# Attention over keys: score tiles in two alternating pairs of banks, queries' keys placed by DMA

## The reference

```
# causal self-attention (fourth sublayer)
q, k, v = split(x @ W_attn + b_attn)            # 16 heads of 8
s = q k^T / (sqrt(8) * temperature) + slope_h * (key - query), key <= query
y = softmax(s) v ;  out = y @ W_proj + b_proj

# cross attention (fifth sublayer)
q = x @ Wq^T ; k, v = ctx @ Wk^T, ctx @ Wv^T    # 16 heads of 8
s = q k^T / sqrt(8), masked where mask[b, key] == 0
out = (softmax(s) v) @ Wo^T
```

## Time and profile before

| | us |
|---|---|
| median of three runs | 1710.38 |
| profiled execution | 1718.98 |
| its span | 1717.2 |
| TensorE (PE) busy | 1404.5 (82%) |
| VectorE (DVE) busy | 1283.2 (75%) |
| ScalarE (ACT) busy | 1015.6 (59%) |
| GpSimd (POOL) busy | 746.1 (43%) |

### The profile page before, as it was taken

How to read it: one execution, slowest core, us unless ns; L and a number is a source line. 1 busy time by engine, 2 the same in 40 slices (tenths; PEclk the granted TensorE clock), 3 DMA queues, 4 the chain that set the end, 5 groups by cost and what they waited for, 6 DMA issues and landing times.

```text
span 1717.2 us, 62575 instructions
## 1 busy us (share of the span) xinstructions
PE 1404.5 (82%) x26438; PEld 907.4 (53%) x26438; DVE 1283.2 (75%) x2645; ACT 1015.6 (59%) x1749; POOL 746.1 (43%) x1471
## 2 busy tenths in 40 slices
PE   4788788878885776777767777999999998989897
PEld 2455455555554443444334444666666666666676
DVE  2345556664453899899988886999999999999966
ACT  2465565666543444444456666777777777777755
POOL 1334334444243565766566664334343333223223
PEclk8688688898775678677655557999999999999999
DMA  7000000000000000000000000000000000000012
GB/s 189 2 2 2 2 3 2 2 3 2 2 2 2 20 15 21 14 15 15 16 1 2 1 1 2 2 3 3 2 3 3 15 15 22 15 22 15 3 32 69
DMA packets 28664, 24.22 MB, mean 14 GB/s; under 512 B 3676, under 2 KB 23906, under 8 KB 28386
## 3 DMA queue, kind: packets, MB, share of 16 engines
q1 hardware_dynamic: 28386, 20.21, 4.3%
HBM read 15.94 MB, written 4.19 MB: 12 GB/s over the span
## 4 chain that ended last, share of the span: by engine, by line
PE 29%; issue 27%; ACT 17%; POOL 17%; DVE 9%; SPq 0%; DMA 0%; POOLq 0%; ACTq 0%; DVEq 0%
PE keys_T L577 7%; ACT keys_pexp L662 5%; POOL gla_low L1102 4%; PE keys_E L473 3%; DVE cross_mx L338 3%; ACT ffn_hqT L1813 2%; POOL gla_yg L1126 2%; ACT keys_pT L644 2%; ACT xs L305 2%; PE keys_E L516 2%; PE ffn_OUT L1774 2%; POOL gla_sq L1119 2%; PE keys_O L584 2%; DVE cross_sums L946 2%; PE keys_S L319 1%
## 5 line engine op out<-in xcount | busy, mean ns | idle before, releaser
L644 ACT ACTIVATE keys_pT<-keys_T 128x512 f32<-128x512 f32 x256 | 152.3, 595 | 107.5 <-PE keys_T L577 104.0
L328 POOL TENSOR_SCALAR keys_spread<-keys_kT,keys_heads 128x512 f32<-128x512 f32 x128 | 86.7, 695 | 260.4 <-ACT keys_kT L608 260.4
L338 DVE TENSOR_REDUCE keys_mx<-keys_S 128x16 f32<-128x1024 f32 x128 | 156.5, 1222 | 39.7 <-PE keys_S L543 25.0
L577 PE MATMUL keys_T<-ident_sb,keys_pexp 128*128 128x128 f32 x1024 | 165.3, 284 | 22.5 <-ACT keys_pexp L662 18.5
L577 PEld LDWEIGHTS keys_T<-ident_sb,keys_pexp 128*128 128x128 f32 x1024 | 112.9, 141 | 98.4 <-ACT keys_pexp L662 50.5
L341 DVE TENSOR_TENSOR keys_pe_in<-keys_S,keys_mx 128x1024 f32<-128x1024 f32 x128 | 156.7, 1224 | 4.4
L1506 DVE COPY_PREDICATED gla_at<-gla_node,gla_GP 128x256 f32<-128x256 int32 x128 | 64.6, 505 | 103.8 <-ACT gla_at L1381 100.5
L662 ACT ACTIVATE keys_pexp<-keys_pe_in 128x1024 f32<-128x1024 f32 x128 | 134.2, 1049 | 0.0
L930 ACT ACTIVATE cross_pexp<-cross_pe_in 128x1024 f32<-128x1024 f32 x64 | 67.4, 1053 | 103.0 <-DVE cross_pe_in L341 102.9
L1119 POOL TENSOR_TENSOR gla_sq<-gla_o 128x512 f32<-128x512 f32 x32 | 33.3, 1039 | 217.9 <-ACT gla_o L1389 217.8
L697 DVE RECIPROCAL keys_rinv<-keys_O 128x128 f32<-128x128 f32 x128 | 120.4, 941 | 0.6 <-issue 0.2
(11 more groups left out here) (278 smaller groups left out, 3720.3 us busy)
## 6 DMA issues: line engine op xcount, KB each, us to landing
context<-in_ctx_T SPq DMA_DIRECT2D x32, 256.0 KB, 2.7
xs<-in_x SPq DMA_DIRECT2D x8, 512.0 KB, 7.3
out_x<-xs SPq DMA_DIRECT2D x16, 256.0 KB, 2.3
keys_mask_q<-keys_mask_b SPq DMA_DIRECT2D x64, 1.0 KB
keys_bias_right_f<-in_alibi_right SPq DMA_DIRECT2D x1, 512.0 KB, 4.0
ffn_w<-in_L_ffn_w_gate_T SPq DMA_DIRECT2D x1, 256.0 KB, 4.9
ffn_w<-in_L_ffn_w_up_T SPq DMA_DIRECT2D x1, 256.0 KB, 5.0
ffn_w<-in_L_ffn_w_down_T SPq DMA_DIRECT2D x1, 256.0 KB, 5.7
```

The lines of the kernel that those rows point to most:

```text
L328: nc.gpsimd.tensor_scalar(spread[:, :, :, j, :].rearrange("q t s k -> q (t s) k"), flat.rearrange("q (a k) -> q a k", k=SEQ), heads[:, j:j ...
L338: nc.vector.tensor_reduce(m, quads(S), X, ALU.max).then_inc(c["mx"], 1)
L577: last = nc.tensor.transpose(T[:, j * P:(j + 1) * P], pexp[:, t % 2, (4 * half + j) * P:(4 * half + j + 1) * P], sh.ident[:, :])
L644: nc.scalar.activation(pT[:, t % 2, 4 * half:4 * half + 4, :].rearrange("q n k -> q (n k)"), T[:, :], ACT.Copy).then_inc(c["pT"], 1)
```

## The change

`S` becomes two tiles of two banks, `S[0]` and `S[1]`, used by even and odd tiles. Scores wait for the subtraction of the tile two before. The scores are four products instead of eight: 64 rows (eight heads) by 64 output rows, 512 columns each. `spread` has OH = 8 places per row instead of 4; its zeros are written once, by GpSimd in the stage ffn, and stay. For each group SP copies each head's eight rows of `kT` into their place: 16 copies of eight rows of 2 KB, SBUF to SBUF. TensorE's first scores of a group wait for all 16, ScalarE's next writing of the same `kT` buffer too. GpSimd no longer multiplies. The mask is added by four products of 512 columns instead of eight of 256 (and copied to two rows instead of four), the bias by two of 512 instead of four of 256. VectorE's two instructions on the scores read the same number of elements, now contiguous. Clearing `vz` moves from the stage cross to ffn. The attribute `staging_read` in the diff is not called by anything.

```diff
+def zeroed(ap):
+    return ap.rearrange("q j n -> q (j n)")
+
+def place_heads(eng, sems, spread, rows, p):
+    for h in range(H):
+        eng.dma_start(spread[h * HD:(h + 1) * HD, p, h % OH, :], rows[h * HD:(h + 1) * HD, p, :]) \
+            .then_inc(sems[p], 16)
+
+def tensor_scores_halves(nc, S, still, spread, t, stop=True):
+    for s in range(2):
+        for a in range(2):
+            rows, at = slice(64 * a, 64 * a + 64), (2 * t + s) * SEQ
+            last = nc.tensor.matmul(S[s * SEQ:(s + 1) * SEQ, a * 512:(a + 1) * 512].rearrange("q (j k) -> q j k", k=SEQ),
+                                    still[rows, s * SEQ:(s + 1) * SEQ], spread[rows, :, at:at + SEQ],
+                                    start=True, stop=stop)
+    return last
+
+def vector_softmax_in_halves(nc, eng, c, S, mx, pe_in, g, t):
+    pp = t % 2
+    c.await_tile(eng, "scores", g, t)
+    x = S[pp][:, :].rearrange("q (h k) -> q h k", k=SEQ)
+    nc.vector.tensor_reduce(mx[:, pp, :], x, X, ALU.max).then_inc(c["mx"], 1)
...
-        spread = sb("spread", [P, 2, G, 2, QH, SEQ])
+        spread = sb("spread", [P, 2, OH, GW])
...
-        S = bank("S", 4)
+        S = [bank(f"S{i}", 2) for i in range(2)]
...
-        PREP, ZEROS = 9, 1
+        PREP, ZEROS = 9, 3
...
         @stage.on("sync")
         def _(sp):
             sp.wait_ge(c["prep"], PREP)
             sh.context_read(sp)
-            for n in range(NG):
+            def context(n):
                 g, p = NG + n, n % 2
                 if n >= 2:
                     c.free_group(sp, "v_done", g, 1)
                 sp.dma_start(cT[:, p, :], am["ctx_T"][:, bass.ds(n * GW, GW)]).then_inc(c[f"ctx{p}"], 16)
+
+            def masks(n):
+                g, p = NG + n, n % 2
                 if n >= 2:
                     c.free_tile(sp, "scores", g, G - 1)
-                for r in range(4):
-                    sp.dma_start(mask_q[32 * r:32 * r + 1, p, :, :, :].rearrange("q t s k -> q t (s k)"),
+                for a in range(2):
+                    sp.dma_start(mask_q[64 * a:64 * a + 1, p, :, :, :].rearrange("q t s k -> q t (s k)"),
                                  mask_b[n * G:(n + 1) * G, :]).then_inc(c[f"mask{p}"], 16)
+
+            context(0)
+            masks(0)
+            context(1)
+            masks(1)
+            for g in range(2 * NG):
+                c.await_nth(sp, "kT", g, 1, 1)
+                if g == 0:
+                    sp.wait_ge(c["zeros"], ZEROS)
+                c.free_tile(sp, "scores", g, G - 1)
+                place_heads(sp, (c["spread0"], c["spread1"]), spread, kT, g % 2)
+                if NG <= g < 2 * NG - 2:
+                    masks(g - NG + 2)
+                    context(g - NG + 2)
 
         @stage.on("gpsimd")
         def _(pool):
             def prepare(stage_, g):
-                if stage_ == 1 and g == 8:
+                if stage_ == 2 and g == 4:
                     nc.gpsimd.memset(vz[:, :, :, :, :, :], 0.0).then_inc(c["zeros"], 1)
+                if stage_ == 2 and g in (7, 10):
+                    nc.gpsimd.memset(zeroed(spread[:, (g - 7) // 3, :, :]), 0.0).then_inc(c["zeros"], 1)
...
-                if part == (3 if causal else 1):
-                    c.await_nth(pool, "kT", g, 1, 1)
-                    c.free_tile(pool, "scores", g, G - 1)
-                    pool_spread(nc, pool, c, spread[:, p, :, :, :, :], kT[:, p, :], heads)
...
                 if t == 0:
-                    c.await_nth(pe, "spread", g, QH, QH)
+                    pe.wait_ge(c[f"spread{p}"], (g // 2 + 1) * 16 * H)
                     c.await_nth(pe, "qT", g, 1, 1)
...
-                c.free_last(pe, "sub", g, t, 1)
-                tensor_scores(nc, S, qT[:, p, t * TILE:(t + 1) * TILE], spread[:, p, t, :, :, :], stop=False)
...
+                c.free_last(pe, "sub", g, t, 2)
+                tensor_scores_halves(nc, S[t % 2], qT[:, p, t * TILE:(t + 1) * TILE], spread[:, p, :, :], t, stop=False)
+                for a in range(2):
+                    if masked:
+                        for s in range(2):
                             last = nc.tensor.matmul(
-                                S[s * SEQ:(s + 1) * SEQ, r * 512:r * 512 + QH * SEQ].rearrange("q (j k) -> q j k", k=SEQ),
...
+                                S[t % 2][s * SEQ:(s + 1) * SEQ, a * 512:(a + 1) * 512].rearrange("q (j k) -> q j k", k=SEQ),
+                                mask_one[64 * a:64 * a + 1, :],
+                                mask_q[64 * a:64 * a + 1, p, t, s, :].unsqueeze(1).to_broadcast([1, OH, SEQ]),
                                 start=False, stop=True)
-                else:
...
+                    else:
+                        last = nc.tensor.matmul(S[t % 2][:, a * 512:(a + 1) * 512], bias_left[:, :],
+                                                bias_right[:, a * 512:(a + 1) * 512], start=False, stop=True)
...
             def keys(g, p):
                 c.await_nth(act, "k_done", g, 1, 1)
-                c.free_group(act, "spread", g, QH)
+                if g >= 2:
+                    act.wait_ge(c[f"spread{p}"], g // 2 * 16 * H)
```

More of the change, by code:

```diff
@@ L401, in attention_over_keys @@
         c.new(*NORM_SEMS, "weights", "zeros", "prep", "bo", "ctx0", "ctx1", "mask0", "mask1", "xr",
-              "xT_done", "xT", "k_done", "kT", "q_done", "qT", "spread", "v_done", "v", "scores", "mx", "sub", "exp",
+              "xT_done", "xT", "k_done", "kT", "q_done", "qT", "spread0", "spread1", "v_done", "v", "scores", "mx", "sub", "exp",
               "pT_done", "pT", "pv", "rinv", "oT")
@@ L526, in scores @@
                 if t == 0:
-                    c.await_nth(pe, "spread", g, QH, QH)
+                    pe.wait_ge(c[f"spread{p}"], (g // 2 + 1) * 16 * H)
                     c.await_nth(pe, "qT", g, 1, 1)
                     if masked:
-                        pe.wait_ge(c[f"mask{p}"], (g - NG - p) * 32 + 64)
-                c.free_last(pe, "sub", g, t, 1)
-                tensor_scores(nc, S, qT[:, p, t * TILE:(t + 1) * TILE], spread[:, p, t, :, :, :], stop=False)
-                if masked:
-                    for s in range(2):
-                        for r in range(4):
+                        pe.wait_ge(c[f"mask{p}"], (g - NG - p) * 16 + 32)
+                c.free_last(pe, "sub", g, t, 2)
[3 more added lines that the diff above has]
+                        for s in range(2):
                             last = nc.tensor.matmul(
-                                S[s * SEQ:(s + 1) * SEQ, r * 512:r * 512 + QH * SEQ].rearrange("q (j k) -> q j k", k=SEQ),
-                                mask_one[32 * r:32 * r + 1, :],
-                                mask_q[32 * r:32 * r + 1, p, t, s, :].unsqueeze(1).to_broadcast([1, QH, SEQ]),
+                                S[t % 2][s * SEQ:(s + 1) * SEQ, a * 512:(a + 1) * 512].rearrange("q (j k) -> q j k", k=SEQ),
+                                mask_one[64 * a:64 * a + 1, :],
+                                mask_q[64 * a:64 * a + 1, p, t, s, :].unsqueeze(1).to_broadcast([1, OH, SEQ]),
                                 start=False, stop=True)
-                else:
-                    for r in range(4):
-                        last = nc.tensor.matmul(S[:, r * 512:r * 512 + QH * SEQ], bias_left[:, :],
-                                                bias_right[:, r * QH * SEQ:(r + 1) * QH * SEQ], start=False, stop=True)
+                    else:
+                        last = nc.tensor.matmul(S[t % 2][:, a * 512:(a + 1) * 512], bias_left[:, :],
+                                                bias_right[:, a * 512:(a + 1) * 512], start=False, stop=True)
                 last.then_inc(c["scores"], 1)
@@ L705, in slot @@
                 if n := back(g, p, t, 0, 2 * NG):
-                    vector_softmax_in(nc, dve, c, S, mx, pe_in, n[0], n[2])
+                    vector_softmax_in_halves(nc, dve, c, S, mx, pe_in, n[0], n[2])
                 if n := back(g, p, t, 3, 2 * NG):
@@ L2237, in decoder @@
         ffn = quantised_ffn(nc, sh, of("L0_ffn_"), cross)
+        sh.staging_read = lambda eng: (eng.wait_ge(ffn.c["prep"], 1), eng.wait_ge(keys.c["prep"], 9))
         sh.context_read = lambda eng: eng.wait_ge(cross.c["k_done"], NG)
```

7 lines of the change are left out of this document (5 added, 2 removed).

## The result

The changed kernel took 1973.47 us in the median of four runs (1971.13 to 1981.21), the kernel before 1712.24 us in the same comparison. The ratio is 1.155, with a 95% interval from 1.147 to 1.164: 261 us slower, forecast 240. The profiled execution took 1981.21 us, its span is 1979.4.

What follows compares the result with a forecast made beforehand. The stage was taken to run on a chain through TensorE. Causal 42, masked 192 and clearing 6 us made 240 us more: 1950 us on the median's scale, chance 0.57, range 1800 to 2065.

Steps and rivals of the forecast that it cites:

- The queue order (part 3, masked): Masked groups: the next group's copies stand behind masks and context in SP's queue; 14 stalls of 8.8 us.
- The price of a copy: SP's placing: 0.605 us an issue, landing 2.0 us, so 11.1 us until all 16 have landed.
- Rival A: SP's placing: a copy issues in 0.35 us, masked stall 5.0 us; 1873 us, chance 0.18.
- rival D: SP's placing: copies fit in TensorE's 3.9 us of other work, leaving scores and clearing; 1755 us, chance 0.05.
- Scores (part 1): TensorE's score products: +0.4 us a tile causal, +0.65 masked; net 1.1 and 1.3 us a group.
- Rival C: TensorE's scores: 64-row pieces run by twos, costing 0.86 us more again; 2030 us, chance 0.06.
- The removed wait: TensorE's scores waiting for the subtraction two tiles back instead of one: worth nothing, since that wait wasn't binding.
- The causal half: Causal groups: placing late by 1.5 us, plus 1.1 for scores; 2.6 x 16 = 42 us.
- The clock in the masked half: TensorE in masked groups: clock at half for 6.8 us after each gap, costing 3.4 us a group.
- Rival B: Masked groups: clock stays low, costing 10.5 us instead of 3.4; + 99 us, 2049 us, chance 0.12.
- the signs: Expected in the trace: about 30 keys_S waits, masked groups 30 to 31 us, causal 20.7, clock below 1.00 only masked.
- Clearing (part 4): GpSimd: clearing vz moves from cross to feed-forward, two clears are added; 6 us, between 0 and 12.

Runs made afterwards that it cites:

- Experiment 1: Changed kernel with SP issuing the mask copies one group earlier, right behind the previous group's placing: 1797.02 us, ratio 1.049.
- experiment 6: Changed kernel with each of the 16 copies moving 512 B a row instead of 2 KB: 1961.64 us.
- experiment 9: Changed kernel with GpSimd spreading keys, bias or mask written first, and score products streaming 256 of 512 columns: 1697.55 us.
- experiment 3: Changed kernel with GpSimd spreading keys, and scores waiting for the subtraction of the tile just before: 1738.64 us, ratio 1.016.
- experiment 7: Changed kernel with ten 512-column products on TensorE ahead of its wait for the placing, in groups 17 to 31: 1973.03 us.
- 5: Changed kernel with mask copies one group earlier in SP's queue and the odd heads' copies issued by GpSimd: 1743.65 us, ratio 1.019.
- 2: Changed kernel with GpSimd spreading the keys by multiplications and SP's queue as before the change: 1736.89 us, ratio 1.014.
- 8: Changed kernel with GpSimd spreading keys, bias or mask written first and scores added to it: 1743.19 us.

## Why the prediction was right, step by step

**The queue order (part 3, masked) was right.** It was forecast at 14 stalls of 8.8 us out of a chain of 12.7 us less 3.9. The boundary above shows 14.3 us less 3.5; most gaps are 10.4 to 10.5 us, the longest 11.5. Experiment 1 took out 176 us by moving nothing but this.

**The price of a copy was 10% low.** I took 0.605 us from the masks; the placing copies start 0.67 us apart, whether 2 KB or 512 B a row (experiment 6). The landing of 2.0 us was right to 0.02. So in the causal groups it was 12.0 to 12.1 us from the keys to the scores in more than half of them and up to 12.8 in the others, where I had 11.1: 1 us or more a group, about 30 us in all. Rival A's 0.35 us an issue and rival D's hidden issues are both refuted by this number. The Trainium skill (DMA: Bandwidth & Descriptors, Issuing engines are not separate DMA queues) says that initiating a transfer is usually small relative to the transfer itself. It is not so for these copies: one issue takes 0.67 us against a landing of 2.0, and the 16 in a row take 16 x 0.67 = 10.7.

**Scores (part 1) were right in size.** Forecast +0.40 us a tile causal: measured 1.02 - 0.62 = 0.40. Forecast +0.65 masked: scores to masks 1.02 against 0.48, masks to weighting 0.34 against 0.28, +0.60. The 0.14 for the changed shape is in there: causal grew by 0.40, but the step from scores to masks by 0.54. Net per group I had 1.1 causal (measured 1.0) and 1.3 masked (measured 0.7): the masked slots had more slack than the two waits that I subtracted. Rival C, pieces that run by twos, is out by experiment 9.

**The removed wait was worth nothing**, as forecast; experiment 3 shows it for the new scores.

**The causal half was too low: 42 us forecast, 4.74 x 16 = 76 measured.** The stall was forecast at 1.5 us and is 2.8; the dearer copies explain 1 us of the 1.3. Nearly as large is a step that I left at nothing: the clock. I had let it fall only in the masked half. With stalls of 2.6 to 3.4 us, spells of 0.50 for 3.4 us came in 11 of the 15 groups behind them, and the first tile's slot then took 6.0 us instead of 4.5. Mean clock between 1200 and 1300 us was 0.97. That is about 1 us a group.

**The clock in the masked half was too high: 3.4 us a group forecast, 2.0 measured** (experiment 7). It stayed at half for 10.2 us, longer than the 6.8 that I assumed, but in the group above 1567.3 to 1573.2, 5.9 us of them, lay inside the gap, where they cost nothing; the other 4.3 us at half rate lose 2.1. Rival B, a clock that stays at half through the groups, didn't occur.

**That the sums came so close is in part luck.** A masked group with a gap was forecast 1.3 + 8.8 + 3.4 = 13.5 us longer. It measured 12.9 (30.73 less 17.80): 0.7 for the scores, 2.0 for the clock, and the rest, 10.2, for the stall. So a stall 1.4 us too low hid a clock 1.4 us too high. Masked sum: 192 forecast, 183 measured; causal 42 and 76. The mechanism was right, the stall was too low everywhere, and the two errors of the clock nearly cancel. Of the signs, causal groups of 20.7 us and a clock below 1.00 in the masked half only did not come: they were 23.1 us in most groups, and the clock fell there too. One sum of the range is wrong: 2049 + 21 is 2070, not 2065. And the row of 57 short waits on "issue" is of PEld, the loading of weights for the scores, not of the products themselves.

**Clearing (part 4)** was forecast at 6 us. From the last cross scores to the first keys the changed kernel took 186.9 us against 184.3, and the cross stage, now without its 5.2 us clear, 296.6 instead of 299.3 from the last instruction of gla to its last scores. So the clears as such cost nothing net. The first group's placing, 12.2 us from keys to scores against 9.5, was not covered: 2.7 us. The stage starts at 1053.2 us in the one profile and 1054.2 in the other, so what lies ahead of it explains none of the 259 us.

By the medians, the loss then divides so: 176 us for the masks ahead of the copies in SP's queue (with the clock that goes with it), 53 to 60 us for 16 copies in one queue in the causal half, also with its clock (experiment 1 against 5 and 2), 25 to 31 us for the new scores (2 and 5 against the kernel before). By the length of the stage in the profiles it is 174, 55 to 57 and 28 to 30 us. Of the last, 25.5 us are the columns (the stage of 8 less that of 9). What stays open is why a copy inside SBUF with eight rows costs 0.67 us to issue on SP, where a mask costs 0.61 and most loads from memory 0.43; only its count and its bytes were varied. That GpSimd issued the same copies at 0.53 us speaks against the transfer itself; no run tests it further.

## What to carry to other kernels

Before a step is moved onto a queue, write down what stands ahead of it there and what those entries wait for: a wait that was harmless in front of an early prefetch becomes a stall when something urgent is queued behind it, here 176 of 261 us, mended by reordering two lines. Count transfers, not bytes, when they are small, and multiply by the issue time of the queue. Fewer, larger pieces on TensorE were no saving here, since four ran at once where eight had, each with twice the columns: 1.02 us to the next product instead of 0.62. Before double buffering, look in the trace for the wait for the buffer: here there was none, and two tiles were worth nothing.

## What the runs showed that I had not expected

- With a TensorE gap of 2.6 to 3.4 us once in 23 us, the granted clock showed 0.50 for a 3.4 us spell in 11 groups of 15; with gaps of 1.8 to 2.2 us (experiment 7), in seven of 14. With gaps of 10 to 11 us and TensorE busy 62 to 67% in the mean, the clock came back each time and stood at 1.00 for 17 to 20 us of every 31. In the feed-forward stage, 70% busy between 900 and 1000 us, it stood at 0.50 for 205 us. In these rows the mean busy share doesn't tell the clock.
- GpSimd's queue issued the same small copies inside SBUF faster (0.53 us each) than SP's (0.67 us).
- Writing the bias first and adding the scores to it was worth 0.32 us a causal group with the new scores, 0.10 with the old.
